# A graph-attention loop: a chunk's four slots summed by one VectorE reduction over five slots of the row buffer instead of by TensorE identity products

## The reference, cut to what matters

```python
xw = (x @ W).reshape(n_nodes, H, C)
logits = leaky_relu(al_s[src] + al_d[dst], 0.2)
m = segment_max(logits, dst);  e = exp(logits - m[dst])
denom = segment_sum(e, dst);   alpha = e / denom[dst]
out = segment_sum(alpha[:, :, None] * xw[src], dst)
```

## Time and profile before

| | us |
|---|---|
| median of 3 runs | 5414.55 (5406.74 to 5415.93) |
| the profiled execution's own time | 5453.07 |
| its span, first to last instruction | 5451.5 |
| POOL busy | 2788.5 (51%) |
| PE busy | 2676.4 (49%) |
| DVE busy | 2371.4 (44%) |
| ACT busy | 595.3 (11%) |

### The profile page before, as it was taken

The page is one execution under the profiler, slowest core; times in us unless marked ns, Lnnn a source line. Parts: engine busy times, 40 slices in busy tenths (PEclk is TensorE's granted clock), DMA queues, the critical chain, the costliest instruction groups (busy, mean ns, idle before and its releaser), DMA issues. The chain is left out here.

```text
span 5451.5 us, 59123 instructions
## 1 busy us (share of the span) xinstructions
PE 2676.4 (49%) x13804; PEld 1949.4 (36%) x13804; DVE 2371.4 (44%) x7341; ACT 595.3 (11%) x1968; POOL 2788.5 (51%) x2942
## 2 busy tenths in 40 slices
PE   1666774254555545546455555555543333333334
PEld 1555543133333333335333333333433323323333
DVE  5888512434444444443344444444423333333333
ACT  2222400120000000003000000000020000000001
POOL 2000021366666666662666666666446666666663
PEclk9667877567766776778666666676765555555555
DMA  2222564033333333332433333333312221221222
GB/s 62 107 95 95 235 213 182 21 84 90 92 92 90 92 89 89 93 88 41 89 90 90 91 92 90 92 88 91 70 32 48 46 48 47 46 47 48 47 46 22
DMA packets 182670, 451.06 MB, mean 83 GB/s; under 512 B 99516, under 2 KB 101378, under 8 KB 177773
## 3 DMA queue, kind: packets, MB, share of 16 engines
q0 software_dynamic: 122928, 318.15, 23.8%
q1 hardware_dynamic: 47214, 128.68, 6.4%
q10 hardware_dynamic: 12384, 2.25, 0.2%
HBM read 392.07 MB, written 57.21 MB: 82 GB/s over the span
## 5 line engine op out<-in xcount | busy, mean ns | idle before, releaser
L498 POOL DMA_INDIRECT rows_all<-gat_tab,ell_list x2664 | 2524.4, 948 | 1473.0 <-issue 859.3
L1007 PE MATMUL banks<-rows_all,ident 128*128 128x264 f32 (+1 forms) x5328 | 1864.9, 521 | 2146.2 <-PEq L121 1627.2
L1007 PEld LDWEIGHTS banks<-rows_all,ident 128*128 128x128 f32 x5328 | 1345.7, 294 | 2665.3 <-issue 2462.1
L1606 DVE TENSOR_TENSOR rows_all<-rows_all,banks 128x1024 f32<-128x1024 f32 (+1 forms) x666 | 684.8, 1042 | 136.5 <-issue 62.0
L1580 DVE COPY lrel<-m_all 128x8 f32 x666 | 129.0, 194 | 1311.0 <-issue 1115.6
L1557 DVE TENSOR_TENSOR acc<-acc,banks 128x264 f32 (+1 forms) x675 | 259.7, 385 | 700.8 <-issue 346.7
L793 ACT ACTIVATE banks<-ex_in 128x40 f32<-128x40 f32 x666 | 138.3, 208 | 3731.8 <-ACTq L121 2194.0
L1550 DVE TENSOR_TENSOR acc<-acc,banks 128x264 f32 (+1 forms) x675 | 257.3, 381 | 118.8 <-issue 113.7
L863 PE MATMUL banks<-rows_all 128*128 128x52 bf16 x4992 | 189.9, 203 | 150.5 <-PEq L121 145.6
L498 POOL DMA_INDIRECT edges<-sw_d,edge_pick x28 | 32.4, 1156 | 411.9 <-POOLq L121 399.9
L863 PEld LDWEIGHTS banks<-rows_all 128*128 128x128 bf16 x4992 | 179.1, 108 | 175.5 <-issue 173.7
(11 more groups left out here) (275 smaller groups left out, 1974.1 us busy)
## 6 DMA issues: line engine op xcount, KB each, us to landing
rows_all<-gat_tab,ell_list POOLq DMA_INDIRECT x2664
x_t<-adj_d SPq DMA_DIRECT2D x11, 3328.0 KB
y_t<-adj_d SPq DMA_DIRECT2D x11, 3328.0 KB
adj_d<-x_t SPq DMA_DIRECT2D x7, 3328.0 KB, 10.3
adj_d<-y_t SPq DMA_DIRECT2D x6, 3328.0 KB, 10.1
ell_list<-ell_d SPq DMA_DIRECT2D x222, 7.5 KB
acc<-key_d SPq DMA_DIRECT2D x1, 1664.0 KB, 6.4
acc<-vec_d SPq DMA_DIRECT2D x1, 1664.0 KB
```

The source lines that it names most:

```text
L498: return g.indirect_dma_start(out=dst, out_offset=None, in_=table, in_offset=bass.IndirectOffsetOnAxis(ap=idx, axis=0))
L1007: last = t.matmul(sum_ps[u % SUMS][:, 0:width], ident[:, :], rows[u][:, r * width:(r + 1) * width], start=(r == 0), stop=(r == SLOTS - 1))
L1606: v.tensor_tensor(msg, msg, exp_ps[u][:, 0:SLOTS, :].unsqueeze(3).to_broadcast([P, SLOTS, HEADS, c]), ALU.mult)\
```

## The change: what it does

The loop no longer uses TensorE. The room of a chunk in the row buffer grows from four rows to five. VectorE's new `fold(u)` comes where the product was: it writes the shrunk sums of the chunk's tile into the fifth row (instead of back into `acc`), multiplies the four slots as before, and then sums the five rows by one `tensor_reduce` into `acc`. The reduction reads the buffer as "p w r": for each of the 264 (136) columns the five values lie one row apart. `weigh` loses the shrinking, the adding and the kept tile numbers, and each of its instructions now waits for the one before. `rows_free` is counted up by ScalarE's first exponential of a chunk, and starts with 4 instead of 6 counts (`LAG = 2`). The reset of the shrink factors goes.

```diff
-LAG = 3
+LAG = 2
...
-        rows_all = sb("rows_all", [P, RING * SLOTS * max(gat_row)])
+        rows_all = sb("rows_all", [P, RING * (SLOTS + 1) * max(gat_row)])
...
-                for u in range(RING - LAG, RING):
-                    last = s.activation(shrink[u], zero_t[:, 0:HEADS], ACT.Exp)
-                last.then_inc(shrink_reset, 1)
...
                         take(act, exp_in)
-                        s.activation(exp_ps[u], ex_in[:, :, :], ACT.Exp)
+                        s.activation(exp_ps[u], ex_in[:, :, :], ACT.Exp).then_inc(rows_free, 1)
...
-                with pe.Fori(0, rounds) as it:
-                    for u in range(RING):
-                        take(pe, msg_ready)
-                        for r in range(SLOTS):
-                            last = t.matmul(sum_ps[u % SUMS][:, 0:width], ident[:, :], rows[u][:, r * width:(r + 1) * width],
-                                            start=(r == 0), stop=(r == SLOTS - 1))
-                        last.then_inc(summed, 1)
-                        take(pe, summed)
-                        pe.sem_inc(sum_made, 1)
-                        pe.sem_inc(rows_free, 1)
...
-            for u in range(RING):
-                signal(rows_free)
+            signal(rows_free, RING - LAG)
...
+                row_h = [rows[u][:, 0:SLOTS * width].rearrange("p (r h q) -> p r h q", h=HEADS, q=c + 1) for u in range(RING)]
+                kept = [rows[u][:, SLOTS * width:(SLOTS + 1) * width].rearrange("p (h q) -> p h q", h=HEADS) for u in range(RING)]
+                by_slot = [rows[u][:, 0:(SLOTS + 1) * width].rearrange("p (r w) -> p w r", w=width) for u in range(RING)]
...
                         v.tensor_copy(lrel[:, SLOTS, :], plane(m_all[:, now, :]))
-                        scored = link.mark(v.tensor_tensor(score[:, :, :], row_h[u][:, :, :, c],
-                                                           sd[:, now, :].to_broadcast([P, SLOTS, HEADS]), ALU.add))
-                        was = tiles[u - LAG] if u >= LAG else was_kept[u]
-                        shrunk = shrink_sums(before_u, was)
-                        link.wait(scored)
...
-                        added = add_sums(before_u, was, shrunk)
...
+                        link(v.tensor_tensor(score[:, :, :], row_h[u][:, :, :, c], sd[:, now, :].to_broadcast([P, SLOTS, HEADS]), ALU.add))
+                        link(v.scalar_tensor_tensor(lrel[:, 0:SLOTS, :], score[:, :, :], LRELU_SLOPE, score[:, :, :], ALU.mult, ALU.max))
+                        link(v.tensor_reduce(plane(m_all[:, now, :]), lrel[:, :, :].rearrange("p r h -> p h r"), AX.X, ALU.max))
+                        v.tensor_tensor(ex_in[:, :, :], lrel[:, :, :], m_all[:, now, :].to_broadcast([P, SLOTS + 1, HEADS]), ALU.subtract)\
+                            .then_inc(exp_in, 1)
...
+                    def fold(u, tile):
+
+                        at = sums[:, bass.ds(tile, 1), :].rearrange("p a (h q) -> p (a h) q", h=HEADS)
+                        v.tensor_tensor(kept[u], at, shrink[u].unsqueeze(2).to_broadcast([P, HEADS, c + 1]), ALU.mult)
+                        msg = row_h[u][:, :, :, 0:c]
+                        link(v.tensor_tensor(msg, msg, exp_ps[u][:, 0:SLOTS, :].unsqueeze(3).to_broadcast([P, SLOTS, HEADS, c]), ALU.mult))
+                        link(v.tensor_reduce(tile_of(sums, tile), by_slot[u], AX.X, ALU.add))
...
                         if u + 1 < RING:
                             weigh(u + 1, tiles[u + 1])
-                        msg = row_h[u][:, :, :, 0:c]
-                        v.tensor_tensor(msg, msg, exp_ps[u][:, 0:SLOTS, :].unsqueeze(3).to_broadcast([P, SLOTS, HEADS, c]), ALU.mult)\
-                            .then_inc(msg_ready, 1)
+                        fold(u, tiles[u])
                         if u + 2 < RING:
                             tiles.append(known_tile(u + 2))
...
-                for u in range(RING - LAG, RING):
-                    tile = kept_tile(u)
-                    link.wait(add_sums(u, tile, shrink_sums(u, tile)))
```

More of the change, by code:

```diff
@@ L62 @@
 SILU_STEPS = ((0, 2), (2, 6), (6, STEPS))
-SUMS = 3
 PAIRS = T // PAIR
@@ L241, in program @@
         ell = [ell_list[u // LISTED][:, u % LISTED * CHUNK:(u % LISTED + 1) * CHUNK] for u in range(RING)]
-        rows_all = sb("rows_all", [P, RING * SLOTS * max(gat_row)])
-        rows = [rows_all[:, u * SLOTS * max(gat_row):(u + 1) * SLOTS * max(gat_row)] for u in range(RING)]
+        rows_all = sb("rows_all", [P, RING * (SLOTS + 1) * max(gat_row)])
+        rows = [rows_all[:, u * (SLOTS + 1) * max(gat_row):(u + 1) * (SLOTS + 1) * max(gat_row)] for u in range(RING)]
         zero_row, junk_a = rows_all[0:1, 0:NP + 1 + P], rows_all[:, 0:NP]
@@ L298, in program @@
         T_ps = [banks[:, 2 + u, :] for u in range(2)]
-        sum_ps = [banks[:, 4 + u, :] for u in range(SUMS)]
         exp_ps = [banks[:, (0, 1, 7)[u % 3], u // 3 * 64:u // 3 * 64 + (SLOTS + 1) * HEADS].rearrange("p (r h) -> p r h", h=HEADS) for u in range(RING)]
@@ L998, in _ @@
                         strip += 1
-                for u in range(RING - LAG, RING):
-                    t.matmul(sum_ps[u % SUMS][:, 0:width], ident[:, :], no_sums[:, 0:width], start=True, stop=True).then_inc(sum_made, 1)
-                rounds = pe.value_load(meta[0:1, 0:1], min_val=1, max_val=CHUNKS // RING)
-                with pe.Fori(0, rounds) as it:
-                    for u in range(RING):
-                        take(pe, msg_ready)
-                        for r in range(SLOTS):
-                            last = t.matmul(sum_ps[u % SUMS][:, 0:width], ident[:, :], rows[u][:, r * width:(r + 1) * width],
-                                            start=(r == 0), stop=(r == SLOTS - 1))
-                        last.then_inc(summed, 1)
-                        take(pe, summed)
-                        pe.sem_inc(sum_made, 1)
-                        pe.sem_inc(rows_free, 1)
                 def turn_means(step, u, turn):
@@ L1144, in _ @@
             signal(tops_ready)
-            link(v.memset(no_sums[:, :], 0.0))
             for l in range(3):
@@ L1563, in known_tile @@
                     return chunk_tile(u)
[L1565 to L1571, removed]
                 with dve.Fori(0, rounds) as it:
-                    tiles, row_h = [], [rows[u][:, 0:SLOTS * width].rearrange("p (r h q) -> p r h q", h=HEADS, q=c + 1) for u in range(RING)]
                     def weigh(u, tile):
@@ L1578, in weigh @@
                         signal(ticks["dve"])
-                        now, before_u = bass.ds(tile, 1), (u - LAG) % RING
+                        now = bass.ds(tile, 1)
                         v.tensor_copy(lrel[:, SLOTS, :], plane(m_all[:, now, :]))
-                        scored = link.mark(v.tensor_tensor(score[:, :, :], row_h[u][:, :, :, c],
-                                                           sd[:, now, :].to_broadcast([P, SLOTS, HEADS]), ALU.add))
-                        was = tiles[u - LAG] if u >= LAG else was_kept[u]
@@ L1584, in weigh @@
-                        shrunk = shrink_sums(before_u, was)
-                        link.wait(scored)
-                        bent = link.mark(v.scalar_tensor_tensor(lrel[:, 0:SLOTS, :], score[:, :, :], LRELU_SLOPE, score[:, :, :], ALU.mult, ALU.max))
-                        if u >= RING - LAG:
-                            link.mark(v.tensor_copy(tile_kept[0:1, u:u + 1], ell[u][0:1, TILE_AT:TILE_AT + 1]))
-                        added = add_sums(before_u, was, shrunk)
-                        link.wait(bent)
@@ L1596, in weigh @@
                             signal(ell_free)
-                    was_kept = [kept_tile(u) for u in range(RING - LAG, RING)]
-                    tiles += [known_tile(0), known_tile(1)]
+                    def fold(u, tile):
[4 more added lines that the diff above has]
+                        link(v.tensor_reduce(tile_of(sums, tile), by_slot[u], AX.X, ALU.add))
@@ L1600, in _ @@
+                    tiles = [known_tile(0), known_tile(1)]
                     weigh(0, tiles[0])
```

6 lines of the change are left out of this document (1 added, 5 removed).

## The result

The kernel after takes 5675.36 us (median of 4 runs, 5668.31 to 5676.36), the kernel before beside it 5412.43 (5406.74 to 5415.93): a ratio of 1.0484, interval 1.0468 to 1.0500. Slower, as forecast, but by 263 us where the sum said 88. The profiled execution of after, 5676.36, is like its other runs; that of before lay 40 above its median. From profile to profile the kernel lost 223 us.

A forecast was written before the change was run, and what follows sets the result against it. Stalls under the gather stream, pausing GpSimd, were taken to bound the loops, with VectorE becoming the wide layers' bound: wide +123, narrow -35, other stages 0, so +88 on the median 5414.55, rounded 5505 us; range 5340 to 5680.

The forecast's parts named there:

- R = 2.5, narrow 1.36: VectorE's new five-row reduction: 2.5 us per chunk in wide layers, 1.36 in the narrow one.
- Rival A: The reduction costs about a dense one, up to 2.1 us, so VectorE keeps up: 5355 us, chance 0.20.
- The round as a sum, 22.85 + 6R: VectorE's wide round of six chunks: 22.85 us plus six reductions of R each, 37.85 us at R = 2.5.
- the wait for the first chunk's exponentials: VectorE at a round's start: 1.12 us, made of 0.92 idle and a 0.20 instruction.
- the reset of the shrink factors: Its removal lets VectorE enter the wide loops earlier, about 10 and 15 us behind the first gather.
- TensorE's and VectorE's see-saw: In the loops before, gathers slow other engines' instructions, GpSimd lacks room and pauses: 6.0 us per chunk, not 5.01.
- The narrow layer, -35: Layer 2's loop keeps its pauses, every five chunks instead of four, and gets 35 us shorter.
- Rival B: TensorE's hand-over alone made the pauses; the narrow loop runs at GpSimd's 5.01 us per chunk: 5330 us, chance 0.08.
- Other stages 0: Stages behind the loops, where TensorE comes in idle: at most +2 us a layer, put at 0.
- From the profile to the median: The same +88 us on the profiled execution (5453 to 5541) and on the median (5414.55, rounded to 5505).
- The tile number, 0.96 in four chunks: VectorE's read for chunk u + 2, now exposed behind the reduction: 0.96 us with the copy's start, in 4 of 6 chunks.
- rival C: Gains and slower wide layers balance, reduction near 2.2 us: no change, 5415 us, chance 0.06.

The follow-up runs named there:

- experiment 6: Kernel after, its reduction reading values 1, 2 or 4 elements apart instead of a row, denominators set to 1: 5006.80, 5004.23 and 5438.18 us.
- Experiment 1: Kernel after with one Exp on a scratch tile ahead of ScalarE's loop, so the activation table is loaded there: 5342.26 us.
- `b_again`: Kernel before, unchanged, run once more with a profile: 4766.31 us.

## Why the prediction was right or wrong

- *R = 2.5, narrow 1.36.* Right to 0.01, and for the reason given. Rival A, the dense cost, fell with it; experiment 6 shows what it was about.
- *The round as a sum, 22.85 + 6R.* Right but for one term, the wait for the first chunk's exponentials. 39.38 - 37.85 = 1.53: the table load 1.28, small waits 0.25 (one chunk of a round is 6.25 us and not 6.05). The entries were put at 10 and 15 us; VectorE's first copy comes 6.8 us behind the first gather in both wide layers. Some rounds above the usual 39.4 us (the means are 39.7 and 39.9) cancel that.
- ***The failed step: the reset of the shrink factors.*** The forecast costed its removal at an earlier entry and nothing else ("VectorE no longer waits for the reset"). The reset was also the only Exp ahead of the loop, and so the wait for the first chunk's exponentials was taken over from before as 0.92 us. The earlier trace rows showed the reset, read as an entry time; the row just ahead of it in the same timeline of before has the load, placed once per layer:

```profile
1143.85 1.28 ACT L787 ACT_TABLE_LOAD   x1
```

  Its removal put 1.28 us on the path of every wide round (the wait is 2.14): about 95 of the 131 us by which the wide loops missed. Experiment 1 gave 46.5 + 48.3 = 94.8 back, in a place without stalls. Of the rest, 0.25 x 74 is 19, and some 16 are stalls that the wide loops still meet in the first place (1449.8 to 1441.6, 1458.0 to 1450.1).
- *TensorE's and VectorE's see-saw sets today's 36.0 us a round.* Right for the trace that was read, and not a property of the kernel: the same program ran in 4756 to 4766 us on four chips, with loops of some 1110. There the forecast's own sum with the load is 37 x 39.13 = 1448 us, for 1441.6 and 1450.1 measured. Over loops of 1108.7 and 1111.0 that is a loss of 676; measured 675.
- *The narrow layer, -35.* -26.2. VectorE was no bound, as forecast (27.2 us of work a round against 30.1 of gathers), and the see-saw was left. But the size was partly luck: the sum had pauses of 4.2 us every five chunks, and they came every six, 5.3 us long. Where there is no see-saw it is 0. Rival B, 5.01 us per chunk, fell.
- *Other stages 0.* -4.
- *From the profile to the median.* The forecast put +88 on both. The profiled execution of before was 40 above its median, that of after equal to its own, so 40 of the 263 us lie there. On chips without the stalls the two agree for before as well (4769.99, median 4766.31).
- The sum of the misses: 95 + 19 + 16 + 9 (narrow) - 4 + 40 = 175, of 263 - 88 = 175.
- *The tile number, 0.96 in four chunks.* The idle was right in size (0.92 forecast, 1.00 measured), but only 0.62 of it comes back when the number is read earlier.
- The range (5340 to 5680) held the time, just; rival C fell with A. Of the signs, R and the longer wide loops came true; VectorE's busy time in a wide loop was 1080 us for 1140, those loops 1450 and 1458 for 1380, and the narrow one 1302 for "under 1300".

Open: what makes the stalls of the first traces. The gathers' spacing and length are the same with and without them. What differs is that the other engines' instructions come late, in VectorE's case as some 0.57 between two that wait for nothing. The rows keep arriving: in 12 of the 12.95 us for which VectorE stands in the earlier trace rows, the DMA engines move 57 GB/s (the window's last number), as in the narrow loop of `b_again` (56).

```profile
4291.00:4303.00 12.00, 2.15 (x8) 1.86 (x8) 0.00 (x0) 0.00 (x0) 9.14 (x10) 0.50 0.22 57
```

Whether it is the chip or its state at that time wasn't settled, nor which engine the pauses need.

## What to carry to other kernels

Before removing an instruction that "only initialises", ask what it leaves behind: here an activation table, whose load then moved into the loop, for nothing while VectorE had slack and for 1.28 us a round once it had none. When a change moves work to one engine, write that engine's round as a sum; here the loop was the larger of that and the gathers' pace, and the loss is read against the best the kernel before can do, not only against one trace with stalls in it. A strided fp32 read by VectorE was free at a step of 8 bytes and cost 0.96 us in 1320 elements at 16 bytes and at 1056.

## What the runs showed of the hardware that I had not expected

- The kernel before in 4756 to 4766 us on four chips and in 5412 where it was first run, with gathers of the same length (945 and 948 ns) and spacing; the kernel after in 5435 to 5441 and 5675. The cause is open.
- The price of a stride is a step, not a slope: 1528 ns at 4 and 8 bytes, 2492 at 16, 2490 at 1056.
- A gather's issue takes up to 1.48 us for 0.95 when it starts while VectorE adds two operands of the row buffer, on average 979 ns for 945 in the kernel. The Trainium skill, "Trainium Architecture — The Big Picture", What this means for kernel authors, says that VectorE and GpSimd share a port pair by an exclusive lock; these rows agree in direction, and no run here separates the port from other causes.
